# The first eight heads' scores, minima and exps made inside the last expert tiles of layer zero

## The reference, cut to what matters

```python
# experts of layer 0: 1024 rows, each goes to 4 of 16 experts
gate, up = gate_up[..., ::2], gate_up[..., 1::2]
gate = jnp.minimum(gate, 7.0)
up = jnp.clip(up, -7.0, 7.0)
glu = gate * jax.nn.sigmoid(gate * 1.702)
out = jnp.einsum('etd,edh->eth', (up + 1.0) * glu, down_proj) + down_proj_bias[:, None, :]
# attention of layer 0: 4 batches x 16 heads = 64 heads of 256 x 256 scores, head size 16
scores = jnp.einsum('bhqd,bhkd->bhqk', q, k) / np.sqrt(HEAD_DIM)
scores = jnp.where(causal[None, None], scores, -jnp.inf)
attn = jax.nn.softmax(scores, axis=-1)
out = jnp.einsum('bhqk,bhkd->bhqd', attn, v)
```

## Time and profile before

| | |
|---|---|
| median of three timed runs | 431.97 us (431.07 to 432.36) |
| the profiled execution's own time | 431.09 us |
| its span | 429.3 us |
| PE busy | 411.7 us, 96% of the span |
| DVE busy | 330.6 us, 77% |
| ACT busy | 236.6 us, 55% |
| POOL busy | 216.7 us, 50% |
| granted clock of PE, mean over the span | 0.986 |

### The profile page before, as it was taken

One profiled execution on the slowest core, in us unless ns is written; L12 is line 12 of the kernel. 1 busy time (PEld: TensorE's weight loads), 2 busy tenths in 40 slices (PEclk: granted clock), 3 DMA queues, 4 the chain that ended last, 5 costly groups with the idle time before them and its releaser, 6 DMA issues.

```text
span 429.3 us, 10086 instructions
## 1 busy us (share of the span) xinstructions
PE 411.7 (96%) x3213; PEld 319.1 (74%) x3213; DVE 330.6 (77%) x1135; ACT 236.6 (55%) x596; POOL 216.7 (50%) x208
## 2 busy tenths in 40 slices
PE   8999999999999999899999979999999999999995
PEld 4856999889999999766666668547777776566684
DVE  5886889989977766769999998866676766644896
ACT  3283243334533343689999962555676766633731
POOL 2114587777734322077886420067676670477720
PEclk9899999999999999969999999999999999999999
DMA  7947988889999998139877977024555552333312
GB/s 230 395 153 271 329 272 257 269 248 287 290 314 307 291 310 285 64 79 257 179 149 183 232 269 242 1 58 136 165 172 169 166 178 97 97 98 111 99 61 73
DMA packets 42275, 84.17 MB, mean 196 GB/s; under 512 B 7137, under 2 KB 27105, under 8 KB 41585
## 3 DMA queue, kind: packets, MB, share of 16 engines
q1 hardware_dynamic: 30656, 60.99, 43.1%
q0 software_dynamic: 9936, 20.85, 19.0%
q10 hardware_dynamic: 1632, 1.71, 1.2%
HBM read 65.81 MB, written 15.60 MB: 190 GB/s over the span
## 4 chain that ended last, share of the span: by engine, by line
PE 82%; DVE 13%; issue 2%; DMA 1%; ACT 1%; POOL 1%; DVEq 0%
PE ps L1130 16%; PE ps L1081 8%; PE ps L1146 7%; PE ps L1308 6%; PE ps L1231 5%; PE ps L1108 5%; PE ps L1206 3%; PE ps L909 3%; PE ps L1067 3%; PE ps L925 3%; PE ps L1319 3%; PE ps L1119 2%; PE ps L1276 2%; PE ps L898 2%; PE ps L928 1%
## 5 line engine op out<-in xcount | busy, mean ns | idle before, releaser
L531 POOL DMA_INDIRECT til<-xn_rows,gidx x95 | 97.6, 1027 | 102.5 <-PE ps L1119 40.3
L1130 PEld LDWEIGHTS ps<-til,experts 128*128 128x128 f32 x752 | 90.9, 192 | 5.4 <-DVE til L1583 2.2
L1130 PE MATMUL ps<-til,experts 128*128 128x128 f32 x752 | 91.9, 275 | 1.5 <-DVE til L1583 1.5
L695 ACT ACTIVATE til<-ps 128x256 f32<-128x256 f32 x47 | 18.0, 383 | 64.4 <-PE ps L1119 63.6
L743 ACT ACTIVATE til<-ps,wtile 128x256 f32<-128x256 f32 x95 | 42.2, 470 | 13.1 <-PE ps L1110 13.1
L796 ACT ACTIVATE til<-til,mxs 128x128 f32<-128x128 f32 (+1 forms) x128 | 48.9, 451 | 0.0
L1146 PE MATMUL ps<-experts,til 128*128 x188 | 48.4, 381 | 0.0
L1675 DVE CUSTOM_DVE_ANT_0 til<-ps,cst 128x128 f32<-128x128 f32 (+1 forms) x128 | 37.8, 352 | 5.2 <-PE ps L1206 4.5
L1083 PE MATMUL ps<-xn,til 128*64 128x192 f32 x192 | 36.3, 332 | 0.0
L1081 PE MATMUL ps<-experts,til 128*64 x192 | 36.3, 332 | 0.0
L1146 PEld LDWEIGHTS ps<-experts,til 128*128 128x128 f32 x188 | 32.1, 190 | 2.8 <-issue 0.3
(11 more groups left out here) (237 smaller groups left out, 913.8 us busy)
## 6 DMA issues: line engine op xcount, KB each, us to landing
experts<-in_gu SPq DMA_DIRECT2D x47, 512.0 KB, 5.7
sorted_rows<-til SPq DMA_DIRECT2D x95, 128.0 KB, 1.9
experts<-in_gu SPq DMA_DIRECT2D x8, 768.0 KB
experts<-in_dn SPq DMA_DIRECT2D x4, 1024.0 KB, 12.6
experts<-in_dn SPq DMA_DIRECT2D x8, 384.0 KB
til<-xn_rows,gidx POOLq DMA_INDIRECT x95
experts<-att SPq DMA_DIRECT2D x44, 32.0 KB
xr<-in_x SPq DMA_DIRECT2D x2, 512.0 KB, 4.1
```

Source lines behind the costliest of these rows:

```text
L531: po.indirect_dma_start(xg[:, t % 4, :], None, xn_dram[s.n], bass.IndirectOffsetOnAxis(ap=gidx[:, t:t + 1], axis=0))\
L1130: mm = pe.matmul(ps[:, b0, m * P:(m + 1) * P], gw[:, j, k * w + m * P:k * w + (m + 1) * P], xgT[:, j % 2, k, :], start=(k == 0), stop=(k = ...
```

## The change

- **The gate uses tanh.** `sigmoid(a g)` becomes `tanh(a g / 2)`; DVE then forms (tanh + 1) * up * gate in one instruction in place of a plain product, and the row weights are halved. The switch of ACT's function table to the sigmoid, and the one back to exp in the last tiles (line 748), are gone.
- **Single banks from tile 32 on** (`ONE_BANK = 32`). `turn` uses bank 0 alone and `down` bank 6 alone. `turn` of tile t then waits for the ACT copy of tile t - 1, and `down` of tile t for `weigh` of tile t - 1, in place of t - 2.
- **Scores of heads 0 to 7** go to the freed banks 1 and 7 and to 4 and 5. They are made in tile steps 36 and 41, between `turn` and `down`. Their minima come on DVE in steps 37 to 40 and 42 to 45, ahead of that step's `gate`, and their exps on ACT one step later each, at the end of the step. They lie in buffers of their own (`pr_early`).
- **The attention starts later in its sequence.** Its pair steps 0 and 1 hold nothing; step 2 starts with the scores of heads 8 to 11 (group 2) and the transposes of pair 0. The minima of heads 8 to 11 come in steps 2 and 3 and their exps in steps 2 to 4. From step 6 on the order is as before.

The core of the diff:

```diff
+        def scores_of(h, tt):
+            return ps[:, h % 4 if h >= EARLY else (1, 4, 5, 7)[h % 4], (slice(0, P), slice(P, 3 * P))[tt]]
+        def turn_bank(t):
+            return t % 2 if t < ONE_BANK else 0
+        def y_bank(t):
+            return 6 + t % 2 if t < ONE_BANK else 6
+        EARLY_TILES = (36, 37, 38, 39, 41, 42, 43, 44)
...
-                    ac.activation(sig[:, j % 2, 0:s.F], gbuf[:, j % 2, :], ACT.Sigmoid, scale=ALPHA)\
+                    ac.activation(sig[:, j % 2, 0:s.F], gbuf[:, j % 2, :], ACT.Tanh, scale=ALPHA / 2)\
...
-                    if s.n == 0 and t == NT0 - 3:
-                        ac.activation(ahead[:, :], ones_e[:, 0:1], ACT.Exp)
...
-                    run_tiles(s, [(0, 1, turn), (0, 1, last_wide), (4, 1, weigh), (1, 1, gate), (1, 1, place_heads), (2, 1, bias_rows)])
+                    run_tiles(s, [(0, 1, turn), (0, 1, last_wide), (4, 1, weigh), (1, 1, gate), (1, 1, place_heads), (2, 1, bias_rows), (2, 1, early_probs)])
...
+            def early_probs(t, j):
+                if t in EARLY_TILES:
+                    head_probs(EARLY_TILES.index(t))
...
                 def turn(t, j):
                     pe.wait_ge(s.xg_full[j], (t + (4 - j)) * 4)
                     if t >= 2:
-                        pe.wait_ge(s.xgT_ready, t - 1)
+                        pe.wait_ge(s.xgT_ready, t - 1 if t <= ONE_BANK else t)
...
                     if t >= 2:
-                        pe.wait_ge(s.y_ready, t - 1)
+                        pe.wait_ge(s.y_ready, t - 1 if t <= ONE_BANK else t)
...
-                        mm = pe.matmul(ps[:, 6 + j % 2, 0:D], hT[0:s.FP, j % 2, k, :],
+                        mm = pe.matmul(ps[:, y_bank(t), 0:D], hT[0:s.FP, j % 2, k, :],
...
                     def first_heads(t, j):
-                        if t == NT0 - 1:
-                            scores(0, 0)
+                        if t in EARLY_TILES[0::4]:
+                            scores(EARLY_TILES.index(t) // 4, 0)
-                    run_tiles(s, [(1, 1, up), (0, 1, turn), (0, 4, experts), (0, 1, begin), (1, 1, weights), (1, 1, bias_rows), (3, 1, first_heads), (3, 1, down)])
+                    run_tiles(s, [(1, 1, up), (0, 1, turn), (0, 4, experts), (0, 1, begin), (1, 1, weights), (1, 1, bias_rows), (0, 1, first_heads), (3, 1, down)])
...
-            run_pairs([(0, 2, lambda n, j: scores(n, j) if n >= 1 else None), (2, 1, turn_probs), (8, 4, turn_rows),
+            run_pairs([(2, ONCE, lambda n, j: scores(2, j)), (0, 2, lambda n, j: scores(n, j) if n >= 3 else None), (2, 1, turn_probs), (8, 4, turn_rows),
...
-                    ve.tensor_tensor(hT[:, j % 2, :, :], ubuf[:, j % 2, :].rearrange("p (m t) -> p m t", m=2),
-                                     sig[:, j % 2, :].rearrange("p (m t) -> p m t", m=2), ALU.mult).then_inc(s.h_ready, 1)
+                    ve.scalar_tensor_tensor(out=hT[:, j % 2, :, :], in0=sig[:, j % 2, :].rearrange("p (m t) -> p m t", m=2), scalar=1.0,
+                                            in1=ubuf[:, j % 2, :].rearrange("p (m t) -> p m t", m=2), op0=ALU.add, op1=ALU.mult).then_inc(s.h_ready, 1)
...
-                    run_tiles(s, [(1, 1, bias_columns), (1, 1, gate), (0, 1, weights(s)), (0, 1, bias_weights)])
+                    run_tiles(s, [(1, 1, bias_columns), (1, 1, early_smallest), (1, 1, gate), (0, 1, weights(s)), (0, 1, bias_weights)])
```

More of the change, by code:

```diff
@@ L169, in build_program @@
         pr = [til[:, 384 * n:384 * (n + 1)] for n in range(6)]
+        pr_early = [xn_free[:, 384 * n:384 * (n + 1)] for n in range(4)]
         prT = [til[:, 384 * n:384 * (n + 1)] for n in range(6, 9)] + [big[:, 14336 + 384 * n:14336 + 384 * (n + 1)] for n in range(5)]
@@ L188, in build_program @@
         fours = [(rou, big)[n // 2][:, n % 2 * 1024:(n % 2 + 1) * 1024].rearrange("p (k n) -> p k n", k=TOPK) for n in range(4)]
+        pr_early = [rou[:, 2048 + 384 * n:2048 + 384 * (n + 1)] for n in range(4)] + pr_early
         ftanh, fsil, oTs = (rou[:, at:at + 512].rearrange("p (t n) -> p t n", t=2) for at in (2048, 2560, 3072))
@@ L679, in turn_and_project @@
                     top_exp(s)
-                ac.activation(ahead[:, :], ones_e[:, 0:1], (ACT.Sigmoid, ACT.Silu)[s.n])
+                ac.activation(ahead[:, :], ones_e[:, 0:1], (ACT.Tanh, ACT.Silu)[s.n])
                 for i in range(copied, NTT - 1):
@@ L781, in tiles, with head_probs, probs @@
                 if s.n == 0:
[L782 removed]
+                    run_tiles(s, [(0, 1, turn), (0, 1, last_wide), (4, 1, weigh), (1, 1, gate), (1, 1, place_heads), (2, 1, bias_rows), (2, 1, early_probs)])
                 else:
                     run_double_tiles([(0, 1, turn_two), (0, 1, last_wide), (1, 1, copy_down), (1, 1, gate_two), (2, 1, weigh_two), (3, 3, row_silu)])
+            def head_probs(h):
+                ac.wait_ge(s_mx, h * 2 + 2)
+                for tt, cols in ((0, slice(0, P)), (1, slice(P, 3 * P))):
+                    ins = ac.activation(probs_of(h)[:, cols], probs_of(h)[:, cols], ACT.Exp,
+                                        bias=min_of(h)[:, tt:tt + 1], scale=-1.0)
+                ins.then_inc(s_exp, 1)
+            def early_probs(t, j):
+                if t in EARLY_TILES:
+                    head_probs(EARLY_TILES.index(t))
             turn_and_project(L[0])
             tiles(L[0])
[L790 to L796, removed]
[L797 to L799 removed]
+            def probs(half, first=6):
+                return lambda p, j: head_probs(2 * p + half) if p >= first else None
             def probs_turned_act(p, j):
@@ L1202, in scores @@
                 at = n // 4 % 2 * SEQ
-                for tt, cols in ((0, slice(0, P)), (1, slice(P, 3 * P))):
+                for tt in range(2):
                     for r in range(4):
                         rows = slice(32 * r, 32 * r + DH)
-                        mm = pe.matmul(ps[:, r, cols], heads_qk[n // 8][rows, 0, n % 4, at + tt * P:at + (tt + 1) * P],
+                        mm = pe.matmul(scores_of(4 * n + r, tt), heads_qk[n // 8][rows, 0, n % 4, at + tt * P:at + (tt + 1) * P],
                                        heads_qk[n // 8][rows, 1, n % 4, at:at + (tt + 1) * P], start=True, stop=True)
```

58 lines of the change are left out of this document (39 added, 19 removed).

## The result

The changed kernel took 446.98 us (median; 442.47 to 449.42), the kernel before 431.79 beside it: a ratio of 1.030 (1.026 to 1.034). Foretold were 443.0, in a range of 438 to 450. A second set of runs gave 443.53 against 433.03, 1.022 (1.018 to 1.025). The change costs 2 to 3%, 10 to 15 us.

The account below looks back on a forecast made before the run. The prediction took the tile loop to be bound by PE alone; 12.9 (down waits) + 0.85 (last two down products) - 2.4 (start of attention) = +11.3 us gave 443.3 us, stated as 443, range 438 to 450.

Parts of the forecast that it names:

- The ring: Tile loop: each down product waits for ACT's weighing behind the copy, 1.17 us in eleven steps, +12.9 us (11.6 to 14.3).
- The refill: Tile loop, after PE's wait in each step: drained products take 1.86 us in place of 1.79, 0.07 more.
- Transposes in one bank, tanh gate, minima and exps: Tile loop: the single transpose bank costs nothing; the other items hide in ACT's and DVE's idle time.
- Scores in the hole: Steps 36 and 41: two score groups, 0.87 us of PE each, fit PE's 1.17 us wait and add nothing.
- The tail: Last two down products, tiles 45 and 46: they wait for ACT's weighing, +0.85 us (0.4 to 1.2).
- The seam: Last down product to group 3's scores: -2.4 us if the clock falls, -4.7 if it stays high; -2.4 taken.
- From there on the same distances as before: Attention from group 3's scores on: unchanged distances, since POOL's last first-batch gather is issued over ten microseconds before its sum.
- The sum: Whole kernel: 12.9 + 0.85 - 2.4 = +11.3 us, 443.3 on the median, stated as 443.
- The rival without a ring: Tile loop: weighing always done before the down product, steps stay 2.87 us; -3.8 us, 428; chance 0.05.

Follow-up runs that it names:

- `weigh` first: The changed kernel with ACT's weighing of tile u - 4 placed ahead of the copy of tile u, in all steps; 433.82 us, ratio 1.001.
- the repeated run: The changed kernel once more, without an edit, against the kernel before; 443.53 us, ratio 1.022.
- half gathers: The changed kernel with ACT's weighing ahead of the copy, and 16 of layer zero's 32 gathers; 464.96 us, no ratio.
- loads later: The changed kernel with ACT's weighing ahead of the copy, and three SyncE loads issued after the attention's first row sum; 468.03 us, ratio 0.999.
- half gathers again: The changed kernel with ACT's weighing ahead of the copy and 16 of 32 layer zero gathers, run once more; 466.53 us, ratio 1.001.

## Why the prediction was right, and where it was not

**The ring: right.** 11 x 1.17 = 12.9 us were foretold; it is 11 x 1.21 = 13.3, in the changed kernel and in the one with the single down bank alone. `Down` came 154.88 - (153.55 + 0.22) = 1.11 us late (1.10 foretold). The refill was larger: from `down` to the next products 0.97 us and not 0.86, 0.11 where I had 0.07. That the copy ahead of `weigh` makes the ring, the experiment with `weigh` first shows: the nine holes of the loop are gone by that one edit. The idle time that I foretold, 1.1 us in eleven steps, reads as 0.95 in nine of them, since the records have each group end a little after the next could start, and in steps 36 and 41 the scores fill it.

**Transposes in one bank, tanh gate, minima and exps: right.** No wait of PE in the tile loop comes from any of them. With `weigh` first the steps with minima and exps in them are 2.87 us, so they need no cover either.

**Scores in the hole: right, with one price too low.** With the ring, steps 36 and 41 are no longer than the others. Without it I priced a group at 0.87, and it costs 1.06: in the rows above the scores start 0.31 us after the transposes (`down` otherwise 0.22), take 0.87, and `down` takes 0.97 in place of 0.86. So the rival without a ring was too kind to itself, by 0.4 us.

**The tail: right.** 0.85 foretold. 14.18 - 11 x 1.21 = 0.87.

**The seam: the right range, the wrong end.** I took -2.4, the clock falling, and kept -4.7. The profiled run had -4.68 at full clock, the repeated run -3.11 with the clock at 0.57 for some 4 us. Even with the fall the gain was 0.7 larger than I had it, since in that run all up to pair 2's transposes (4.53 us) still ran at the full clock. One execution's rows could not say which end would come; two executions of one kernel differ in it.

**"From there on the same distances as before": wrong.** This is the step that failed. I had read the earlier trace rows so: the first batch's last gather is issued at 195.91, its sum runs at 206.66, so there is slack of ten microseconds. But the sum needs the landing, not the issue: in the changed kernel the chain has 9.21 us for the fourth sum's last gather. And POOL's gathers don't move with the pairs: in all six profiles of the undisturbed occasions the first one starts 3.3 to 3.5 us after E, since it waits for the last tile's rows. Only the sums move with the pairs. Before, the first sum ran 26.02 us after E and didn't wait; in the changed kernel it ran 22.30 after E, and 0.88 of that was a wait. It had therefore come 26.02 - 21.42 = 4.6 us early, by the seam's gain, and the slack had been 3.7. By the landings of the other two runs with a short seam (22.53 with `weigh` first, 24.30 in the repeated run) it would be 3.5 and 1.7, so it differs between executions. The fourth sum waited 1.71. Of the 3.35 us given back, 2.4 lie ahead of the fourth sum, and the table of six profiles has them go with the sums' waits. The other 0.9 lie behind it, where kernels with the old seam have as much, so I don't count them to the change. That the waits take the gain back is shown by those distances and by the chain, which runs through the gathers up to the fourth sum; the test without the gathers' waits gave nothing, since its runs were the disturbed ones.

**The sum.** On the spans: 13.3 + 0.87 - 4.7 + 3.35 = 12.8, and +3.95 ahead of step 36 give the 16.8 between the two profiled executions. The forecast of 11.3 left out the last term and took the seam at -2.4; these two errors, +3.35 and -2.3, nearly cancel, which is luck. The ratio of 1.0255 that it amounts to lies between the 1.030 and the 1.022 of the two sets.

**The rival without a ring** was worked out as -3.8 us, 428. As a kernel (`weigh` first) it is even with the one before: 3.0 in the loop and tail where I had 0.9 (1.74 - 0.87), and 2.8 given back. Most of the 2.1 us in the first of these come from the tail: with a single bank the last two down products wait for ACT (0.75 and 0.67 us) without the ring too, and this rival had left that out. In the other versions on that base nothing shows a kernel that beats the one before.

## What to carry to other kernels

When a buffer loses its second half, look at the order on the engine that frees it: what stands ahead of the freeing instruction and waits for the engine that wants the buffer closes a ring. Its price in every step is what the chain from one engine to the other and back takes, both instructions and both hand-overs, less what overlaps (here 1.11 us, and 0.11 for the refill). The cure can be one move in that order and not the buffer.

When a stage is to start earlier, list what in it hangs on another clock than the stage itself (gathers tied to the last tile), measure each slack to the landing and not to the issue, and let the gain end at the smallest.

## What the runs showed of the hardware

PE with nine holes of 0.95 us, one per step of 4.08 us, kept the granted clock at 1.00 for over 40 us. At the old seam holes of 1.41 and 1.00 us were followed by 0.58; in the run with transposes in one bank the fall to 0.50 came already behind the hole of 1.41. At the new seam PE has holes of 0.76, 0.67, 1.03 and 0.73 us in six profiles. In three of them (the changed kernel's first run, `weigh` first, half gathers) the clock then stayed at 1.00, in the other three (the repeated run, loads later, half gathers again) it averaged 0.57 to 0.59 over 4 us from the start of pair 2's transposes on. The Trainium skill, "TensorE: Matmul & The Clock Gate", section "A second HAM failure mode: psum-queue depth-cycling", tells of another kernel, whose cycling through PSUM banks left short idle times often enough that the clock went back and forth; the trace does not agree in the tile loop, and the seam leaves it open.

On two later occasions, on two chips, every kernel here took 33 us longer, and one of these was the chip that had run the kernel before in 433 us. From step 36 to E the time was the same to the hundredth there (35.11 us with the tanh gate alone, 38.13 with half gathers); nearly all of the difference lay behind E. An experiment for one microsecond needs the kernel before beside it, and a look at its absolute time first.
